# Expert rows weighted before they are stored, and a second attention with a new order of its side work

## The chip, the cores and the metric

One core of a Trainium2 chip runs the kernel. Its engines are TensorE (PE in the profile, its weight loads PEld), VectorE (DVE), ScalarE (ACT), GpSimd (POOL) and SyncE (SP), which here only issues transfers. Each runs its own program; semaphores order them. The metric is the device time of one execution in microseconds, median of three runs.

## What is computed

8192 tokens (128 sequences of 64) of 128 values go through four blocks, each added to x:

```python
x = x + L0_xattn(layernorm(x), ctx_1024, ctx_1024, mask)     # 16 heads of 8
x = x + L0_ffn(layernorm(x))       # rmsnorm, 32 experts, top 4, clipped swiglu; returns its input plus the sum
x = x + L1_xattn(layernorm(x), ctx_1024, ctx_1024)           # the same with rotary embedding, no mask
x = x + L1_ffn(layernorm(x))       # 8 experts, hidden 352, top 2, silu gate
# an experts block: y[token] = sum over its k experts of weight[token, k] * expert_k(row[token])
# weight = softmax of the chosen gate logits
```

## The kernel before

All is written by hand: every engine's program, its order and its semaphores. X (64 tiles of 128 tokens) stays in SBUF. The stages run one behind the other: `attention(0)`, `slots(0)`, `invert(0)`, `experts0()`, then the same for layer 1, then `finish()`.

**attention(layer)** takes two tiles (four sequences) an iteration, 32 iterations, in a software pipeline. Each engine has a `body(i, on)` that does pieces of iteration i and of its neighbours (`on(k)` says whether i + k exists; `nx` is i+1, `ex` i+2, `pv` i-1, `pp` i-2). `bodies` writes out the first eight and the last seven, and loops over the rest in pairs.

- SP loads the context and stores the rows for the experts (L380) into `expert_rows`, 512 B each.
- PE: scores (L782) into four banks U_, for layer 0 the next inputs' transposes, values (L838, L844) of pv, projections (L864, L865) of nx into P_, the rows of pp turned (L914), the maxima of i turned (L793) into R_, the scores turned (L807, L819), in layer 1 the rotated projections (L864, L865 again) into M_, nx's values (L875), pv's output (L885, L889) into R_, the gate of pp (L946) into R_, and in layer 1 the transposes of ex's inputs (L857, L859).
- DVE: statistics of ex's X (L497, L502), the four score maxima (L544), a copy of the turned maxima (L551), the division of pv (L584, L586), in layer 1 the rotary products (L592, cosine, then sine) and their sum (L603), normalisation of ex (L518), addition of the output to X (L639), the logits of pp out of PSUM (L559), its output statistics and its top 8 (L572, L576). R_ is one bank for maxima, output and gate, so each waits until the former is read.
- ACT: copies out of PSUM (L734, L683, L740), the exponentials (L659), the experts' rows (L702) and, in layer 1, half of the spreads (L667). A spread copies queries or keys four times, each masked to one head in four.
- POOL: reciprocal roots (`pow`, L424, L448) and what stands around them, spreads (L429: all four heads in layer 0, two in layer 1), and the keeping of the top 8 (L486, L487).

In layer 1 the result of the experts before is still in `slot_results`, one row for each token and chosen expert. POOL's `gather` fetches it for i+4: it copies the indices (L408), then issues eight indirect gathers (L412), four ahead of the spreads and four behind. DVE's `combine(i, k)` adds them to X for i+3 in four steps k, each two operations x = row * weight + x (L535), one tile each; the steps stand between other work (behind L603, behind L518, behind L559, at the end), and each waits for the former.

**slots** ranks the tokens' choices by expert and gives each a slot in tiles of 128 slots; `wts` are the softmax weights. **invert** finds the token of every slot.

**experts0** has 72 groups of four slot tiles. POOL gathers each tile's rows from `expert_rows` (L1354, four a group, four buffers XE), PE turns them (L1415), multiplies (L1453, L1455), turns the hidden values (L1471) and multiplies again (L1488, L1490); ACT copies and does the gelu; DVE clips (L1523, L1525), multiplies (L1530) and copies the result out of PSUM (L1536); SP stores it to `slot_results`. **experts1** does the same for layer 1 with 36 groups, and fetches and weights its own results at its end and in **finish** (L1260, L1276).

## Time and profile before

| | |
|---|---|
| median of 3 runs | 2034.29 us (2033.54 to 2034.76) |
| the profiled execution | 2034.43 us, of which 2032.6 from first to last instruction |
| mean granted TensorE clock | 0.875 |
| busy: PE, DVE, ACT, POOL | 1551.1, 1210.9, 802.7, 1199.5 us |
| slot results gathered, issue to landing | 2.5 us (median) |

The stages in us from the start of the span: first attention to 396, its slots and inversion to 524, first experts to 923, second attention 926 to 1509, slots and inversion to 1568, second experts and finish to the end.

How to read it: a row of a timeline gives the start, the duration, the engine, the line of the kernel and, in brackets, how long the engine was idle before it and what released it. A row "x2" is two instructions. A share of busy time says little here, since the engines wait for each other in turn; the question at each stage is which wait ends last. Matmuls' ends are modelled, so starts are the safer numbers.

### The profile page before, as it was taken

The page shows a single profiled execution, that of the slowest core. Times are in us where ns is not written, and L with a number is a line of the kernel's source. Part 1 is how long each engine was busy: PE and PEld are TensorE (multiplying, and loading weights), DVE is VectorE, ACT ScalarE, POOL GpSimd, SP SyncE. Part 2 cuts the span into 40 slices and gives each one's busy share as a digit, 9 for nine tenths or more (in the row PEclk, how much of TensorE's full clock was granted, in tenths as well). Part 3 has the DMA queues.
Part 4 walks back from the last instruction along what each step waited for, and adds up shares of the span by engine and source line. Part 5 has one row for each costly group of instructions (what it writes and reads, how often), then busy time and mean ns, then how long its engine had stood idle before and what let it go on. Part 6 is the DMA issues. An engine that isn't in the chain of part 4 may idle for free. (4 is left out here: it accounts for less than half of the span.)

```text
span 2032.6 us, 58857 instructions
## 1 busy us (share of the span) xinstructions
PE 1551.1 (76%) x21070; PEld 1134.8 (56%) x21071; DVE 1210.9 (60%) x3027; ACT 802.7 (39%) x1780; POOL 1199.5 (59%) x1657
## 2 busy tenths in 40 slices
PE   1999999609799999982777777787854999998800
PEld 1666666404477777761455555555532777776600
DVE  2677777699455555543788888888768222333312
ACT  1666666516333333321333333333325444444400
POOL 1667666300577777755777777777511634477566
PEclk9999999859899999996888888877775999999955
DMA  5111111000133333362311111111100222233322
GB/s 174 40 32 39 39 39 35 15 2 0 43 104 102 100 97 103 103 78 59 131 47 46 45 47 46 46 46 46 32 12 6 66 60 56 60 88 85 74 63 66
DMA packets 140639, 120.61 MB, mean 59 GB/s; under 512 B 21475, under 2 KB 126731, under 8 KB 140043
## 3 DMA queue, kind: packets, MB, share of 16 engines
q0 software_dynamic: 26112, 53.53, 11.7%
q1 hardware_dynamic: 114206, 65.84, 10.8%
q8 instruction: 55, 0.90, 0.2%
q14 instruction: 26, 0.21, 0.0%
q10 hardware_dynamic: 240, 0.12, 0.0%
HBM read 78.45 MB, written 40.97 MB: 59 GB/s over the span
## 5 line engine op out<-in xcount | busy, mean ns | idle before, releaser
L1354 POOL DMA_INDIRECT arena<-expert_rows,arena x432 | 420.6, 974 | 171.4 <-issue 119.4
L412 POOL DMA_INDIRECT arena<-slot_results,arena x256 | 250.9, 980 | 92.6 <-issue 59.5
L429 POOL TENSOR_TENSOR arena<-arena,head_of 128x1024 f32<-128x1024 f32 (+1 forms) x128 | 187.1, 1482 | 100.4 <-DVE arena L603 52.2
L1694 DVE TENSOR_TENSOR arena<-bank,arena 128x352 f32<-128x352 f32 x144 | 75.5, 524 | 243.9 <-ACT arena L1673 243.8
L1627 PE MATMUL bank<-W,arena 128*128 x576 | 196.8, 465 | 0.9 <-ACT arena L1685 0.9
L1455 PE MATMUL bank<-W,arena 128*128 x576 | 172.9, 396 | 0.0
L659 ACT ACTIVATE arena<-bank 128x512 f32<-128x512 f32 x256 | 132.2, 603 | 101.1 <-PE bank L819 99.2
L544 DVE TENSOR_REDUCE mx<-bank 128x8 f32<-128x512 f32 x256 | 157.8, 678 | 14.5 <-PE bank L782 14.5
L1260 POOL DMA_INDIRECT arena<-slot_results,arena x128 | 122.0, 953 | 55.4 <-issue 26.0
L1523 DVE TENSOR_SCALAR arena<-bank 128x256 f32<-128x256 f32 x144 | 61.1, 424 | 143.8 <-PE bank L1455 143.7
L1641 PEld LDWEIGHTS bank<-W,arena 128*128 128x128 f32 (+1 forms) x864 | 113.3, 191 | 39.4 <-issue 32.2
L1226 PE MATMUL bank<-arena 128*128 128x288 f16 (+1 forms) x384 | 86.1, 394 | 56.7 <-ACT arena L1211 36.3
L946 PE MATMUL bank<-gate_w,arena 128*128 128x32 f32 (+1 forms) x256 | 50.8, 315 | 95.4 <-DVE X L639 94.4
L1641 PE MATMUL bank<-W,arena 128*128 (+1 forms) x864 | 120.8, 276 | 1.9 <-ACT arena L1680 1.9
L535 DVE SCALAR_TENSOR_TENSOR X<-arena,wts,X 128x128 f32 (+1 forms) x256 | 105.2, 451 | 27.2 <-DMA arena<-slot_results,arena 26.0
L734 ACT ACTIVATE arena<-bank 128x512 f32<-128x512 f32 x64 | 38.2, 597 | 206.6 <-PE bank L859 206.6
L1627 PEld LDWEIGHTS bank<-W,arena 128*128 128x128 f32 x576 | 99.5, 193 | 33.0 <-issue 3.1
L1490 PE MATMUL bank<-W,arena 128*128 x576 | 113.8, 318 | 0.0
L584 DVE RECIPROCAL arena<-bank 128x256 f32<-128x256 f32 x64 | 111.8, 1747 | 0.5 <-PE bank L844 0.5
L946 PEld LDWEIGHTS bank<-gate_w,arena 128*128 128x128 f32 x256 | 45.2, 250 | 106.5 <-issue 103.9
L1673 ACT ACTIVATE arena<-bank 128x352 f32<-128x352 f32 x144 | 66.7, 463 | 93.0 <-PE bank L1627 93.0
L782 PE MATMUL bank<-arena 32*64 32x256 f32 x2048 | 97.1, 503 | 4.5 <-POOL arena L429 4.2
(186 smaller groups left out, 3633.0 us busy)
## 6 DMA issues: line engine op xcount, KB each, us to landing
slot_results<-arena SPq DMA_DIRECT2D x108, 256.0 KB
arena<-in_ctx SPq DMA_DIRECT2D x64, 128.0 KB, 2.3
expert_rows<-arena SPq DMA_DIRECT2D x64, 128.0 KB, 2.1
arena<-expert_rows,arena POOLq DMA_INDIRECT x432
arena<-slot_results,arena POOLq DMA_INDIRECT x384, 2.5
W<-in_w SPq DMA_DIRECT2D x1, 4096.0 KB, 12.1
X<-in_x SPq DMA_DIRECT2D x32, 128.0 KB, 2.2
out_x<-arena SPq DMA_DIRECT2D x32, 128.0 KB, 1.8
```

Of the source, the lines that this page charges most:

```text
L412: nc.gpsimd.indirect_dma_start(out=gb[q][:, k * D:(k + 1) * D], out_offset=None, in_=ys, in_offset=bass.IndirectOffsetOnAxis(ap=gi[q][:, k ...
L429: nc.gpsimd.tensor_tensor(dst[i.par].rearrange("p (b j k) -> p b j k", b=4, j=4)[:, :, 0:n, :], src[i.par].rearrange("p (b k) -> p b k", b ...
L535: last = nc.vector.scalar_tensor_tensor(xt, gb[q][:, at:at + D], wts[:, bass.ds(i.n * 2 + j, 1), k], xt, ALU.mult, ALU.add)
L544: nc.vector.tensor_reduce(mx[:].rearrange("p (w c) -> p w c", w=2)[:, :, 32 * r:32 * r + 4], U_[r][:, :].rearrange("p (w j k) -> p w j k", ...
L584: nc.vector.reciprocal(rec, O_[:, 2 * D:4 * D]).then_inc(s["o_recip"], 1)
L659: nc.scalar.activation(Pt[r], U_[r][:, :], ACT.Exp, scale=SCALE).then_inc(s["probs"], 1)
L1260: nc.gpsimd.indirect_dma_start(out=gb[q][:, k * D:(k + 1) * D], out_offset=None, in_=ys, in_offset=bass.IndirectOffsetOnAxis(ap=gi[q][:, k ...
L1354: nc.gpsimd.indirect_dma_start(out=XE[q][:, c * D:(c + 1) * D], out_offset=None, in_=ts, in_offset=bass.IndirectOffsetOnAxis(ap=gi[i.table ...
L1455: last = nc.tensor.matmul(h, XT[i.par][:, c * P:(c + 1) * P], W0a[:, bass.ds(x_e, 1), :], start=False, stop=True, skip_group_check=True)
L1490: last = nc.tensor.matmul(y, AT[pv.par][:, c * P:(c + 1) * P], W0b[:, bass.ds(x_e, 1), :], start=False, stop=True, skip_group_check=True)
L1627: last = nc.tensor.matmul(H_[2 * r + u][:, 0:F1], XT[i.par][:, c * P:(c + 1) * P], W1a[:, bass.ds(x_e, 1), u * F1:(u + 1) * F1], start=Tru ...
L1641: last = nc.tensor.matmul(Y_[j.par][:, d * P:(d + 1) * P], AT[d % 2][0:f, k * P:(k + 1) * P], W1b[0:f, bass.ds(x_e, 1), k * P:(k + 1) * P] ...
```

## The change

In the experts of layer 0 the weights move: `slots(0)` puts each token's four weights and four expert numbers into `pay`, SP stores them behind the token's 128 values in `expert_rows`, whose rows become 136 words (544 B), and `experts0` multiplies a slot's result by its own weight where it left PSUM by a copy before. DVE finds that weight by comparing the row's four expert numbers with the tile's expert, `tile_e`. The experts of layer 1 gather the longer rows too, and keep their weighting at the end.

So the second attention only has to sum four gathered rows. The sum is one reduction and one addition, for i+4, at the end of DVE's body. DVE takes over four small operations of GpSimd. All spreads of layer 1 are made by ScalarE, keys first. The gathers are for i+5 and read `slot` directly; GpSimd's program for layer 1 is written out for every iteration. Rows for the experts, their turning, the gate and its logits are three iterations late instead of two, the choice of the top 8 with them; PE does the gate before nx's values and the output, and the output waits for the logits' copy.

```diff
+ROW = D + 2 * K0
+        pay = sb("pay", [P, TILES, 2 * K0])
+        tile_e = sb("tile_e", [P, SLOT_TILES[0]])
...
-                        sp.dma_start(ts_rows[:, bass.ds(i.n * 2, 2), :],
+                        sp.dma_start(ts_rows[:, bass.ds(i.n * 2, 2), 0:D],
...
-                    def gather(i, half):
+                    def gather(i, k):
+                        if k == 0 and i.n >= 2:
+                            hold(pool, s["combined"], i.n - 1)
+                        for j in range(2):
+                            at, to = i.n * 2 + j, (j * K0 + k) * D
                             nc.gpsimd.indirect_dma_start(
+                                out=gb[i.par][:, to:to + D], out_offset=None, in_=ys,
+                                in_offset=bass.IndirectOffsetOnAxis(ap=slot[:, at, k:k + 1], axis=0),
+                            ).then_inc(gathered[i.par], 16)
...
+                    def body_with_gathers(i, on):
+                        if on(5):
+                            gather(i.at(5), 0)
+                        if on(-2):
+                            scale_outputs(i.at(-2))
+                        if on(5):
+                            gather(i.at(5), 1)
+                        if on(3):
+                            scale_inputs(i.at(3))
+                        if on(5):
+                            gather(i.at(5), 2)
+                        if on(-4):
+                            keep_top(i.at(-4))
+                        if on(5):
+                            gather(i.at(5), 3)
+                    if layer:
+                        for n in range(-5, ITERS + 4):
+                            body_with_gathers(Step(0, n, base), lambda k: 0 <= n + k < ITERS)
...
+                    def combine(i):
+                        q = i.par
+                        hold(dve, gathered[q], (i.half + 1) * 16 * 2 * K0)
+                        nc.vector.tensor_reduce(rows_sum.rearrange("p (i d) -> p i d", i=2),
+                                                gb[q].rearrange("p (i k d) -> p i d k", i=2, k=K0), AX.X, ALU.add
+                                                ).then_inc(s["row_sum"], 1)
+                        hold(dve, s["row_sum"], i.n + 1)
+                        nc.vector.tensor_tensor(tiles(X, i), tiles(X, i), rows_sum.rearrange("p (i d) -> p i d", i=2),
+                                                ALU.add).then_inc(s["combined"], 1)
...
+                    def body_with_sums(i, on):
+                        ex, nx, pv, p3 = i.at(2), i.at(1), i.at(-1), i.at(-3)
+                        if on(3):
+                            hold(dve, s["combined"], i.at(3).n + 1)
+                            stats(i.at(3), small["st_a"], small["mv_a"], "stats_a", "moments_a")
+                        if on(0):
+                            for r in range(UNITS):
+                                score_unit(i, r)
+                            max_rows(i)
+                        if on(-1):
+                            divide(pv)
...
+                            rotate(nx)
+                        if on(-3):
+                            read_logits(p3)
+                        if on(2):
+                            hold(dve, s["rstd_a"], ex.g + 1)
+                            normalise(ex, xn, small["mv_a"], small["rs_a"]).then_inc(s["normed"], 1)
+                        if on(-1):
+                            add_output(pv)
+                        if on(-3):
+                            choose(p3)
+                        if on(-1):
+                            output_stats(pv)
+                        if on(4):
+                            combine(i.at(4))
...
-                            for j in range(pool_heads, 4):
-                                for dst, src in ((Kbd, Kt), (Qbd, Qt)):
+                            for dst, src, done in ((Kbd, Kt, "kbd"), (Qbd, Qt, "qbd")):
+                                for j in range(4):
...
+                    def body_with_rotation(i, on):
+                        ex, nx, pv, p3 = (i.at(k) for k in (2, 1, -1, -3))
+                        if on(0):
+                            scores(i)
+                        if on(-1):
+                            values(pv)
...
+                            projections(nx, P_, wq, wk, s["qk_psum"])
+                        if on(-3):
+                            rows_turned(p3)
...
+                            maxima(i)
+                            turned(i)
...
+                            projections(nx, M_, Wm[:, 8, :], Wm[:, 9, :], s["rot_psum"])
...
+                            gate(p3)
+                        if on(1):
+                            next_values(nx)
+                        if on(-1):
+                            if on(-3):
+                                pe.wait_ge(s["logits"], p3.g + 1)
+                            output(pv)
...
+                            inputs(ex)
...
+                        sp.wait_ge(chain, weighed_at[0])
+                        sp.dma_start(ts_rows[:, :, D:ROW], pay[:]).then_inc(weights_out, 16)
...
+                        if not base:
+                            hold(pool, e["weighed"], i.g - 3)
...
-                            out=XE[q][:, c * D:(c + 1) * D], out_offset=None, in_=ts,
+                            out=XE[q][:, c * ROW:(c + 1) * ROW], out_offset=None, in_=ts,
...
+                    def row_weights(i):
+                        dve.wait_ge(slots_in[i.quad], (i.fourth + 1) * 16 * GROUP)
+                        dve.nop(nofuse=True)
+                        rows = XE[i.quad].rearrange("p (c f) -> p c f", c=GROUP)
+                        ck = lambda v: v.rearrange("p (c k) -> p c k", k=K0)
+                        nc.vector.tensor_tensor(ck(own), rows[:, :, D + K0:ROW],
+                                                tile_e[:, bass.ds(i.n * GROUP, GROUP)].unsqueeze(2)
+                                                .broadcast_to([P, GROUP, K0]), ALU.is_equal).then_inc(e["own"], 1)
+                        dve.wait_ge(e["own"], i.g + 1)
+                        nc.vector.tensor_tensor(ck(own_w), ck(own), rows[:, :, D:D + K0], ALU.mult
+                                                ).then_inc(e["own_w"], 1)
+                        dve.wait_ge(e["own_w"], i.g + 1)
+                        nc.vector.tensor_reduce(row_w[i.quad], ck(own_w), AX.X, ALU.add).then_inc(e["weighed"], 1)
+
                     def body(i, ahead, main, behind):
-                        pv = i.at(-1)
+                        nx, pv = i.at(1), i.at(-1)
+                        if ahead:
+                            row_weights(nx)
...
-                            nc.vector.tensor_copy(YE[pv.par], Y_[:, :]).then_inc(e["y"], 1)
+                            dve.nop(nofuse=True)
+                            nc.vector.tensor_tensor(YE[pv.par].rearrange("p (c d) -> p c d", c=GROUP),
+                                                    Y_[:, :].rearrange("p (c d) -> p c d", c=GROUP),
+                                                    row_w[pv.quad].unsqueeze(2).broadcast_to([P, GROUP, D]), ALU.mult
+                                                    ).then_inc(e["y"], 1)
...
-    ts = nc.dram_tensor("expert_rows", (TOKENS, D), F32, kind="Internal").ap()
+    ts = nc.dram_tensor("expert_rows", (TOKENS, ROW), F32, kind="Internal").ap()
```

## Rows read from the trace of the kernel before

**Rows 1.** Busy us: PE, PEld, DVE, ACT, POOL; then granted clock, DMA.

```profile
926.00:1509.00 583.00, 430.06 (x7968) 307.32 (x7968) 443.69 (x1216) 201.86 (x449) 406.01 (x607) 0.79 0.19 52
```

**Rows 2.** Timeline of DVE, second attention: start, us, instruction, idle before and releaser.

```profile
1210.56 0.42 DVE L551 COPY arena<-bank 128x256 f32<-128x256 f32 x1 [1.28 <-PE bank L793]
...
1214.71 0.69 DVE L603 TENSOR_TENSOR arena<-arena 128x512 f32<-128x512 f32 x1
...
1216.63 1.31 DVE L518 TENSOR_SCALAR arena<-X,arena 128x128 f32 x2
...
1218.39 0.41 DVE L639 TENSOR_TENSOR X<-bank,X 128x256 f32 x1
...
1219.98 0.17 DVE L559 COPY arena<-bank 128x16 f32<-128x16 f32 x1 [1.18 <-PE bank L946]
...
1220.72 0.48 DVE L497 BATCH_NORM_STATS2 arena<-X 128x6 f32 x2
...
1223.65 2.46 DVE L544 TENSOR_REDUCE mx<-bank 128x8 f32<-128x512 f32 x4
...
1227.56 0.42 DVE L551 COPY arena<-bank 128x256 f32<-128x256 f32 x1 [1.45 <-PE bank L793]
```

**Rows 3.** Timeline of PE in the same iteration.

```profile
1210.14 0.38 PE L793 MATMUL bank<-ident,mx 128*128 128x128 f32 x2
...
1212.61 0.70 PE L864 MATMUL bank<-arena,Wm 128*128 128x256 f32 x2
...
1218.95 0.99 PE L946 MATMUL bank<-gate_w,arena 128*128 128x8 f32 x4 [3.25 <-DVE X L639]
```

**Rows 4.** GpSimd by line, 560 to 860 us: busy, mean ns, idle.

```profile
L1354 POOL DMA_INDIRECT arena<-expert_rows,arena x231 | 228.8, 990 | 68.3 <-issue 64.6 <-POOL arena L1337 2.4 <-PE bank L1415 1.2
```

**Rows 5.** Timelines of ScalarE and of GpSimd in the same iteration.

```profile
1215.44 1.70 ACT L667 ACTIVATE arena<-arena,head_of 128x256 f32<-128x256 f32 x4 [0.71 <-DVE arena L603]
...
1215.49 2.12 POOL L429 TENSOR_TENSOR arena<-arena,head_of 128x512 f32<-128x512 f32 x2 [1.15 <-DVE arena L603]
...
1219.11 0.94 POOL L412 DMA_INDIRECT arena<-slot_results,arena  x1 [0.30 <-issue]
```

**Rows 6.** Timeline of DVE, first iterations of the second attention.

```profile
949.69 0.60 DVE L518 TENSOR_SCALAR arena<-X,arena 128x128 f32<-128x128 f32 x2
```

**Rows 7.** Timeline of PE, last iterations of the second attention.

```profile
1486.89 1.12 PE L782 MATMUL bank<-arena 32*64 32x256 f32 x32 [0.28 <-issue]
...
1488.86 1.05 PE L844 MATMUL bank<-arena,den_of 128*32 128x256 f32 x16
```

**Rows 8.** Instructions by line and form, DVE, 1500 to 1600 us.

```profile
L1072 DVE TENSOR_REDUCE arena<-arena 128x64 f32<-128x1024 f32 x2 | 2.4, 1220 | 0.1
...
L1065 DVE TENSOR_TENSOR arena<-bank,arena 128x512 f32<-128x512 f32 x2 | 1.9, 1005 | 0.0
```

**Rows 9.** Busy time of six us behind PE's long gap.

```profile
1219.00:1225.00 6.00, 6.00 (x112) 4.38 (x116) 4.58 (x22) 1.52 (x4) 4.95 (x11) 0.50 0.33 87
```

**Rows 10.** Timeline of PE, first iterations of the second attention.

```profile
972.45 0.69 PE L793 MATMUL bank<-ident,mx 128*128 128x128 f32 x2 [0.58 <-DVE mx L544]
...
976.61 0.70 PE L864 MATMUL bank<-arena,Wm 128*128 128x256 f32 x2
...
997.05 0.66 PE L857 MATMUL bank<-ident,arena 128*128 128x128 f32 x2 [2.39 <-DVE arena L518]
```

**Rows 11.** Timeline of GpSimd, start of the second attention.

```profile
928.45 0.94 POOL L412 DMA_INDIRECT arena<-slot_results,arena  x1 [0.30 <-issue]
```

**Rows 12.** Timelines of DVE, first and last L551 of the second attention.

```profile
973.17 0.42 DVE L551 COPY arena<-bank 128x256 f32<-128x256 f32 x1 [0.78 <-PE bank L793]
...
1491.17 0.42 DVE L551 COPY arena<-bank 128x256 f32<-128x256 f32 x1 [0.60 <-PE bank L793]
```

**Rows 13.** Timelines of PE and of DVE, first experts stage.

```profile
702.94 0.65 PE L1415 MATMUL bank<-ident,arena 128*128 128x128 f32 x4 [0.57 <-DMA arena<-expert_rows,arena]
...
704.89 0.42 DVE L1523 TENSOR_SCALAR arena<-bank 128x256 f32<-128x256 f32 x1 [1.32 <-PE bank L1455]
```

More of the change, by code:

```diff
@@ L360, in bodies @@
                         body(Step(m, c, base), lambda k: True)
-                for n in range(ITERS - 4, ITERS + 3):
+                for n in range(ITERS - 4, ITERS + 4):
                     at(n)
@@ L670, in projections @@
                                         scale=head_of[:, j:j + 1])
+                                last.then_inc(s[done], 1)
                         else:
@@ new lines, in rows_turned, with gate @@
+                    def rows_turned(i):
+                        pe.wait_ge(s["t_ready"], i.g + 1)
+                        for w in range(2):
+                            last = nc.tensor.transpose(M_[:, w * P:(w + 1) * P],
+                                                       t[i.par][:, w * P:(w + 1) * P], ident[:])
+                        last.then_inc(s["tt_psum"], 1)
+                    def gate(i):
+                        pe.wait_ge(s["tt"], i.g + 1)
+                        for w in range(2):
+                            last = nc.tensor.matmul(R_[:, w * n_e:(w + 1) * n_e],
+                                                    tT[i.par][:, w * P:(w + 1) * P], gw, start=True, stop=True)
+                        last.then_inc(s["gate_psum"], 1)
@@ L1543, in experts1 @@
             place[0] = 0
-            XE = [carve(GROUP * D) for _ in range(4)]
+            XE = [carve(GROUP * ROW) for _ in range(4)]
             XT, YE = (carve2(GROUP * D) for _ in range(2))
```

297 lines of the change are left out of this document (138 added, 159 removed).

## Prediction, made before the kernel was run

> **What bounds the kernel now.** I read the page's slices and the busy time by stage first, then one iteration of the second attention on each engine, then the groups of instructions of the first experts stage. The second attention runs from 926 to 1509 us, 583 us for 32 iterations; no engine is full (DVE 444, PE 430, GpSimd 406 us busy) and the granted clock is 0.79 [rows 1]. So the reader should look for a circle of waits. One iteration takes 17.0 us, from one L551 to the next [rows 2]. DVE goes from L551 (1210.56) through the reciprocal, the rotation (L603 ends at 1215.40), a combine, the normalisation (L518), a second combine, and X (L639, ends 1218.80). Only then does PE, idle for 3.25 us, start the gate's matmuls (1218.95) and behind them, in order, the next inputs' transposes, scores, values and projections, until the maxima's transposes free the next L551 [rows 2, 3]. PE's half is 8.5 us, DVE's 8.2 us: the circle alternates, and what stands between L603 and L639, and the gate in front of the inputs, is paid in full.
>
> The first experts stage is bound elsewhere: GpSimd's gathers are busy 228.8 us and between issues 68.3 us of 300 us [rows 4]. It has no room there.
>
> **The change, part by part, in the second attention.** I rebuild the iteration with the new order instead of only subtracting. Let t = 0 be the end of L603.
>
> DVE: read the logits of three iterations before (0.17 us, no wait, since PE has done that gate long before; before, it waited 1.18 us [rows 2]). Then the normalisation: its two L518 took 1.31 us beside GpSimd's spread, but 0.60 us where no spread ran [rows 2, 5, 6]. The spreads leave GpSimd, so I take 0.60: t = 0.65. The Trainium skill (SBUF — State Buffer, the section on the shared port) says that a DVE operation in a two-port mode and a GpSimd operation block each other for the whole instruction; the trace agrees, 1.31 against 0.60 us, and the sum would be the same by either.
>
> PE: the output's matmuls wait for the logits' copy; from L639's end to L946 a release takes 0.15 us, and three matmuls, of which L864's pair is the measure with 0.70, take about 0.7 [rows 2, 3]: they end at t = 1.0. Inputs about 0.8 us more (four transposes; two take 0.38 [rows 3]).
>
> ScalarE now makes all eight copies of the spread. Four took 1.70 us, starting at t = 0.04 [rows 5]. Those of K are first, so the scores can start at t = 1.9, the same moment as the inputs' end; those of Q end at 3.5, long before they are read. Its iteration grows from 6.3 us (202 over 32 [rows 1]) to about 8.2, no bound.
>
> PE from there at full clock: scores and values 3.0 us (1486.89 to 1489.91 [rows 7]), projections about 1.0, rows turned 0.2: ready for the maxima at t = 6.1.
>
> DVE: X at t = 1.1 (0.34 to the next start). Output statistics, choice and input statistics: L497 to L544 is 2.93 us with one pair of combines of 0.6 in it [rows 2], so 2.3; two waits and three little operations that come over from GpSimd, 0.6 (each some 0.1 issued plus a wait). Then the new sum: one reduction of 128x1024 and one addition of 128x256 (0.42 as L639 [rows 2]) instead of eight operations. A contiguous reduction of 128x1024 takes 1.22 us; but this one reads its four terms 512 B apart, and the only operation that reads with such steps, L1065, took 1.005 us for 512 elements where L603 has 0.69 for as many [rows 2, 8]. That is 0.6 ns an element more, so 1.84 us; I take that, because the access is what differs, and keep 1.22 and 2.3 as ends. The Trainium skill (SBUF — State Buffer, its note on cachelines) states that a read which goes to a new 16-byte line each time pays a penalty, which speaks against this reduction; the trace agrees with L1065. Without the rule and without L1065 the sum would be 0.6 us an iteration lower. Together: 1.1 + 0.34 + 2.3 + 0.6 + 2.35 = t 6.7, and the four L544 (2.46 us [rows 2]) end at t = 9.1.
>
> So DVE, not PE, is late at the maxima: PE stands idle from 6.1 to 9.1. Maxima 0.4 us and release, then L551 to L603's end 4.84 us [rows 2]: an iteration of 14.4 us.
>
> **The clock.** That gap of 3.0 us is in a worse place. After the gap of 3.25 us the granted clock is 0.50 for the next 6 us (1.2 instead of 2.4 GHz) [rows 3, 9], and after one of 2.39 us it fell too: L857's pair takes 0.66 us [rows 10]. Before, the slow stretch fell on scores and values. Now it would fall on the maxima's and turned scores' matmuls and the rotated projections, for whose result DVE's sine step waits without slack: L864 and its twin start at 1212.61 and take 1.1 us together, and between 1213.7 and L603 at 1214.71 DVE has only that step. From L793 to L864 is 4.16 us at the low level and 2.47 at the full one [rows 3, 10]: up to 1.7 us an iteration, 2.7 with the projections, 0 if the clock stays. I take 1.2, less than one full slow stretch, since it may not come in every iteration. Period 15.6 us; bounds 13.8 (cheap reduction, full clock) and 17.1.
>
> GpSimd: eight gathers at 1.25 us (0.94 + 0.30 [rows 5]), and what is left of its 12.7 busy us an iteration (406 over 32 [rows 1]) without 7.6 of gathers, 2.12 of spreads and 0.9 of moved small work: 2.1, with gaps 2.3. Together 12.3 us. It starts an iteration when the sum of two tiles earlier is done and has 14.4 or more, so it hides; if it did not, 12.3 is the floor of the period. Writing its program out costs nothing that I can see: the gathers of the stage's first iterations, which are written out already, have the same 0.30 us between them [rows 11]. The gathers' descriptors read `slot` itself instead of a copy.
>
> **Ends of the stage.** Gathers begin at 927.2, one before the row's [rows 11]. DVE's order wants four tile pairs summed before the first scores, not three: 4 x 10.0 + 1.6 = 968, landing 1.7 (the page has 2.5 from a gather's issue), sum 2.35, statistics 1.0, L544 2.5, maxima 0.8: the first L551 at 976.4, before 973.17 [rows 12]. The last three iterations carry no sum, then no statistics, and are short: 6.1 + 0.5 + 4.84 = 11.5 each. The last L551: 976.4 + 28 x 15.6 + 34.5 = 1447.7, before 1491.17 [rows 12]. The drain behind it keeps its chain (values, output, statistics, gate, choice) and pays about 0.5. Gain: 43 us.
>
> **The weighting in the first experts stage.** Rows of 544 B instead of 512 carry weights and experts. DVE's copy of 512 elements out of PSUM becomes a multiplication of as many; L639, an addition with one input in PSUM, and L551, a copy, both take some 0.42 us for 256 [rows 2], so nothing. Three small operations of DVE (0.2 each with their waits) for the next group stand before its clipping; they wait for the same gather that PE waits for, and from that landing (L1415 at 702.94) to the first clipping (704.89) are 1.95 us in which DVE stood idle 1.32 [rows 13], so they hide; without that cover, 0.6 x 72 = 43 us. GpSimd gets one more wait a group, on something an iteration old. As the stage is GpSimd's, anything that lengthens a gather counts 288 times; no row shows a row of 544 B, so -0 (nothing gets shorter) to +0.25 us each is my bound, and I take 0.007, +2 us in all, since the bytes grow by 6% and descriptors by none. The second experts stage gathers 544 B too, under PE. The payload's transfer (8192 pieces of 32 B) has 110 us of slots and inversion behind it. The first attention is unchanged but for stores to rows 544 B apart, for which nobody waits.
>
> **Sum.** The profiled execution took 2034.43 us (span 2032.6), the median is 2034.29. 2034.4 - 43 + 2 = 1993 us.
>
> **Rivals.** (a) The clock stays up or the reduction is cheap: period 13.8 to 14.9, gain 62 to 93: 1943 to 1974, say 1958. For it: PE's work is otherwise dense. Against it: both gaps above. 0.27. (b) The clock falls in every iteration for the whole turned part, or the strided reduction costs 2.3: period 16.4 to 17.1, 2014 to 2034, say 2025. The price is exactly 28 us per 1 us of period. 0.15. (c) Slower: rows of 544 B make GpSimd's gathers longer, in the one stage that it bounds. From 0.15 us a gather (43 us over 288) the gain is gone; at 0.25 us the time is 2063. For it: no slack on GpSimd there [rows 4]. Against: the operation's time has so far been that of its descriptors, 0.94 us undisturbed, from either table. 0.08. (d) The change does not do what it says: the gate, though three iterations late, still holds PE, because the output now waits for the logits' copy, which stands behind the rotation. In my schedule that costs 0.2 us only, as DVE normalises meanwhile; were it a full round trip, 1.2 us more: 2027. 0.04.
>
> **Numbers.** The forecast, 1975 to 2014, has 0.46. The range, to hold 8 in 10, takes most of (a) and (b): 1948 to 2030. Differences of 0.2% (4 us) are about what a measurement tells from none. Faster 0.88: forecast, (a), most of (b) and (d). Same 0.04, from (b). Slower 0.08, (c).
>
> **What would show it.** L551 to L551 in the loop: 15.6 us. L518 as a pair 0.6 us. No DVE wait ahead of L559's successor. The reduction 1.8 us. PE's one large gap ahead of the maxima, about 3 us, and the granted clock low behind it, at the turned scores; the stage's clock near 0.8 again. GpSimd waiting some 2 us an iteration for the sum. Gathers of 544 B at 0.94 us, stage one of the experts unchanged at 5.2 us a group. It is wrong if the gathers lengthen, if the reduction is above 2.3 us, or if ScalarE's spreads, not DVE, are last at the scores.

## The result, and the profile after

The changed kernel takes 2001.8 us (median of 4 runs, 2000.0 to 2005.6) where the kernel before took 2034.5 beside it: ratio 0.984 (95% interval 0.9825 to 0.985), 33 us less. Its profiled execution has a span of 2000.3 us against 2032.6. The forecast was 1993, the range 1948 to 2030.

All of it but about 1 us is in the second attention (the last result of the first experts leaves PSUM at 921.26, before at 922.59). The row below answers to [rows 1], over the same stretch (with us, then busy us of PE, PEld, DVE, ACT, POOL, the granted clock, the DMA share and GB/s):

```profile
926.00:1509.00 583.00, 383.69 (x7987) 283.16 (x7988) 441.93 (x1173) 252.59 (x586) 317.91 (x420) 0.86 0.18 52
```

GpSimd is busy 318 us instead of 406, ScalarE 253 instead of 202, VectorE as before; the clock is 0.86, not 0.79. One iteration of VectorE, the part that answers to [rows 2] (L573 is the old L551, L625 the old L603, L556 the old L518, L630 the old L639, L581 the old L559, L566 the old L544):

```profile
1199.93 0.42 DVE L573 COPY arena<-bank 128x256 f32<-128x256 f32 x1 [0.53 <-PE bank L833]
...
1204.08 0.69 DVE L625 TENSOR_TENSOR arena<-arena 128x512 f32<-128x512 f32 x1
1204.69 0.17 DVE L581 COPY arena<-bank 128x16 f32<-128x16 f32 x1
1204.78 0.59 DVE L556 TENSOR_SCALAR arena<-X,arena 128x128 f32 x2
1205.87 0.42 DVE L630 TENSOR_TENSOR X<-bank,X 128x256 f32 x1 [0.50 <-PE bank L924]
...
1208.10 2.03 DVE L536 TENSOR_REDUCE arena<-arena 128x256 f32<-128x1024 f32 x1
1210.34 0.43 DVE L540 TENSOR_TENSOR X<-X,arena 128x256 f32 x1 [0.21 <-DVE arena L536]
...
1211.93 2.48 DVE L566 TENSOR_REDUCE mx<-bank 128x8 f32<-128x512 f32 x4
1214.95 0.42 DVE L573 COPY arena<-bank 128x256 f32<-128x256 f32 x1 [0.53 <-PE bank L833]
...
1219.60 0.88 DVE L614 SCALAR_TENSOR_TENSOR arena<-bank,bias_t,sin 128x256 f32<-128x256 f32 x2 [1.31 <-PE bank L905]
...
1231.34 0.42 DVE L573 COPY arena<-bank 128x256 f32<-128x256 f32 x1 [0.53 <-PE bank L833]
```

The reader is to see two iterations here, one of 15.0 us (1199.93 to 1214.95) and one of 16.4 (to 1231.34). The logits are read without a wait, the normalisation is down to 0.59 us, and what differs between the two iterations is one wait: 1.31 us before the sine products. TensorE at the same place, which answers to [rows 3]:

```profile
1206.66 1.12 PE L822 MATMUL bank<-arena 32*64 32x256 f32 x32 [0.57 <-ACT arena L706]
...
1210.57 0.38 PE L933 MATMUL bank<-ident,arena 128*128 128x128 f32 x2
1214.47 0.44 PE L833 MATMUL bank<-ident,mx 128*128 128x128 f32 x2 [3.52 <-DVE mx L566]
1214.84 2.01 PE L847 MATMUL bank<-arena 32*64 32x128 f32 x64
1216.59 1.91 PE L859 MATMUL bank<-arena,max_to 32*64 32x256 f32 x32
1218.43 0.70 PE L904 MATMUL bank<-arena,Wm 128*128 128x256 f32 x2
```

TensorE stands idle for 3.52 us before the maxima's transposes, and behind that the turned scores (L847, L859) take 2.01 and 1.91 us. The windows of that stretch and, under it, of the same one in the iteration before, with the columns of [rows 1], show why:

```profile
1214.60:1218.20 3.60, 3.60 (x98) 2.68 (x98) 3.22 (x5) 0.00 (x0) 2.76 (x4) 0.54 0.08 21
1199.50:1203.00 3.50, 3.50 (x104) 2.84 (x104) 3.03 (x5) 0.98 (x3) 2.69 (x4) 1.00 0.07 19
```

The 15.0 us iteration has the full clock, 2.4 GHz, there; the 16.4 us iteration has a granted 0.54, nearly all at 1.2 GHz. The wait before the sine products comes in about two iterations of three, with 1.2 to 2.2 us. Over the 28 iterations behind the first L573 the mean is 16.07 us (17.01 before). The first and the last L573, which answer to [rows 12]:

```profile
975.32 0.42 DVE L573 COPY arena<-bank 128x256 f32<-128x256 f32 x1 [0.78 <-PE bank L833]
...
1458.73 0.43 DVE L573 COPY arena<-bank 128x256 f32<-128x256 f32 x1 [0.59 <-PE bank L833]
```

The last came at 1491.17, so 32.4 us are gained up to here, and the span is 32.3 us shorter: nothing was gained or lost behind it. The gathers of the first experts stage, same columns as [rows 4]:

```profile
L1443 POOL DMA_INDIRECT arena<-expert_rows,arena x232 | 228.6, 985 | 68.6 <-issue 60.9 <-DVE arena L1620 3.4 <-POOL arena L1424 2.4
```

### The profile page after: what moved, and what is told of

Read it like the earlier page. It is cut to its first block and busy times, and to the rows that moved or that the text cites. A ratio compares the mean times of both kernels' runs of the same rounds, so it can differ in the third digit from the quotient of the medians.

```text
span 2000.3 us, 58820 instructions
## 1 busy us (share of the span) xinstructions
PE 1501.8 (75%) x21070; PEld 1109.1 (55%) x21071; DVE 1214.6 (61%) x3147; ACT 850.7 (43%) x1908; POOL 1108.1 (55%) x1465
## 5 line engine op out<-in xcount | busy, mean ns | idle before, releaser
L413 POOL DMA_INDIRECT arena<-slot_results,slot x256 | 247.7, 968 | 192.9 <-DVE X L540 93.9
L698 ACT ACTIVATE arena<-bank 128x512 f32<-128x512 f32 x256 | 132.2, 602 | 224.3 <-PE bank L859 224.3
L566 DVE TENSOR_REDUCE mx<-bank 128x8 f32<-128x512 f32 x256 | 158.4, 681 | 9.6 <-PE bank L822 9.6
L1347 POOL DMA_INDIRECT arena<-slot_results,arena x128 | 122.0, 953 | 55.4 <-issue 26.6
L430 POOL TENSOR_TENSOR arena<-arena,head_of 128x1024 f32<-128x1024 f32 x64 | 119.8, 1893 | 49.1 <-ACT arena L713 49.1
L706 ACT ACTIVATE arena<-arena,head_of 128x256 f32<-128x256 f32 x256 | 105.6, 495 | 38.7 <-DVE arena L625 38.7
L1739 PEld LDWEIGHTS bank<-W,arena 128*128 128x128 f32 x576 | 99.5, 193 | 32.9 <-issue 3.0
L1785 ACT ACTIVATE arena<-bank 128x352 f32<-128x352 f32 x144 | 66.9, 464 | 93.6 <-PE bank L1739 93.6
L833 PE MATMUL bank<-ident,mx 128*128 128x128 f32 x128 | 28.9, 310 | 97.2 <-DVE mx L566 97.2
L1546 PEld LDWEIGHTS bank<-W,arena 128*128 128x128 f32 x576 | 88.6, 194 | 21.5 <-issue 1.4
L1313 PEld LDWEIGHTS bank<-arena 128*128 128x128 f16 x384 | 41.6, 119 | 100.8 <-issue 36.7
L859 PE MATMUL bank<-arena,max_to 32*64 32x256 f32 x2048 | 91.8, 453 | 0.5 <-issue 0.5
```

The lines of the kernel that those rows point to most:

```text
L413: nc.gpsimd.indirect_dma_start(out=gb[i.par][:, to:to + D], out_offset=None, in_=ys, in_offset=bass.IndirectOffsetOnAxis(ap=slot[:, at, k: ...
L430: nc.gpsimd.tensor_tensor(dst[i.par].rearrange("p (b j k) -> p b j k", b=4, j=4), src[i.par].rearrange("p (b k) -> p b k", b=4).unsqueeze( ...
L566: nc.vector.tensor_reduce(mx[:].rearrange("p (w c) -> p w c", w=2)[:, :, 32 * r:32 * r + 4], U_[r][:, :].rearrange("p (w j k) -> p w j k", ...
L698: nc.scalar.activation(Pt[r], U_[r][:, :], ACT.Exp, scale=SCALE).then_inc(s["probs"], 1)
L1313: last = nc.tensor.matmul(total[g][:, 0:NT], by_id[c].rearrange("p (i k s) -> p i k s", i=2, k=K)[:, j, k, :], hot_high[c].rearrange("p (i ...
L1347: nc.gpsimd.indirect_dma_start(out=gb[q][:, k * D:(k + 1) * D], out_offset=None, in_=ys, in_offset=bass.IndirectOffsetOnAxis(ap=gi[q][:, k ...
```

## The experiments

The theory after the result: two terms make 16.07 us. VectorE's own order, with its two waits of 0.5 us for TensorE, takes 15.0, of which 2.67 are the new sum (from L536's start to L540's end), and TensorE's low clock behind its gap adds 1.1 on average. The rivals: the low clock merely coincides with a long iteration; the reduction has cover; the gain came from the gate's new place alone; the longer rows cost something that something else gave back. All ratios are to the kernel before on the same chip; where the text gives a difference between two kernels in us, it is that of their ratios, times 2034.5. "Period" is the mean of the 28 iterations behind the first L573 (or its equal).

| kernel | ratio (95%) | median us | period us |
|---|---|---|---|
| changed | 0.984 (0.9825 to 0.985) | 2001.8 | 16.07 |
| changed, gap filled with 24 matmuls | 0.972 (0.970 to 0.974) | 1978.6 | 14.93 |
| changed, 12 matmuls | 0.983 (0.981 to 0.985) | 2003.8 | 15.84 |
| changed, reduction in address order | 0.972 (0.970 to 0.975) | 1976.9 | 14.99 |
| changed, sum in two additions | 0.967 (0.964 to 0.970) | 1970.8 | 15.03 |
| two additions and 20 matmuls | 0.961 (0.958 to 0.963) | 1954.6 | 14.10 |
| changed, gate put back | 0.996 (0.995 to 0.998) | 2029.9 | 16.83 |
| gate put back and 24 matmuls | 0.979 (0.977 to 0.981) | 1994.0 | 15.35 |
| changed, rows of 768 B | 0.983 (0.981 to 0.985) | 2001.2 | 16.00 |
| before, gap filled with 24 matmuls | 0.987 (0.986 to 0.989) | 2010.1 | 16.08 |
| two additions spread, 10 matmuls | 0.945 (0.943 to 0.947) | 1925.6 | 13.00 |
| two additions spread | 0.944 (0.941 to 0.947) | 1923.6 | 12.90 |

**The clock.** The gap is filled with matmuls into a part of the bank that nobody reads:

```diff
                             pe.wait_ge(s["added"], pv.g)
+                        if on(-2) and on(1):
+                            for _ in range(24):
+                                nc.tensor.matmul(R_[:, 256:512], ones_b[:], sel_of[:, 0:256], start=True, stop=True,
+                                                 skip_group_check=True)
                         if on(0):
                             maxima(i)
```

> The changed kernel, with 24 matmuls of 256 bfloat16 columns, whose result nobody reads, put on TensorE between the wait for the residual and the transposes of the maxima, so that the 3.5 us in which TensorE otherwise idles in every iteration of the second attention are filled. My theory, that the missing 1.2 us between the iterations of 15.0 us at full clock and the mean of 16.2 us are the low clock after that gap: the granted clock of the stage stays at 1.00, the start of L573 returns every 14.9 to 15.2 us in every iteration, and about 29 iterations give back 1.2 us each, some 30 to 35 us, which makes 1965 to 1975 us. Rival one, that the low clock only coincides and the chain through VectorE and the waits on ScalarE is what sets 16.2: within 0.3% of the changed kernel's 2001.8 us. Rival two, that the filler delays the transposes more than it saves (each is 0.11 us at full clock but 0.21 at half): slower, up to 2020 us.

It took 1978.6 us, 24 less than the changed kernel and fewer than the 30 to 35 expected. The period is 1.14 us shorter, 32 us in 28 iterations; but the last three, which have no sum and so no gap, take 39.9 us instead of 33.5, since the idle matmuls stand in their way there (VectorE waits 3.52 and 4.63 us for the maxima), and the first L573 comes 2.2 us later. TensorE in one iteration of it, and the busy time of 1000 to 1400 us:

```profile
1211.70 2.78 PE L1008 MATMUL bank<-sel_of,ones_b 128*128 128x256 bf16 x24
1215.16 0.44 PE L833 MATMUL bank<-ident,mx 128*128 128x128 f32 x2 [0.68 <-DVE mx L566]
1215.53 1.24 PE L847 MATMUL bank<-arena 32*64 32x128 f32 x61
```

```profile
1000.00:1400.00 400.00, 352.00 (x7284) 276.01 (x7272) 344.60 (x922) 204.43 (x475) 248.53 (x332) 1.00 0.20 61
```

The clock is 1.00 throughout (0.90 in that window of the changed kernel), L573 returns every 15.0 us from the sixth iteration on, and the sine products wait no more. The low clock is a cause, worth 1.1 us an iteration; VectorE's path makes 15.0. Half the dose:

> The changed kernel with 12 idle matmuls instead of 24, a dose: 1.3 of the 3.5 us of the gap are filled. 24 made every iteration 15.0 us. If the cost goes by the length of the gap that is left (2.2 us; the two kernels with a shorter sum, whose gap was 2.5 to 2.7 us, kept the clock in about half of their iterations), most iterations are 15.0 us and the time is 1978 to 1986 us; if the whole gap has to be filled, it stays at 1995 to 2002 us.

It did nothing that can be measured against the changed kernel (0.983 against 0.984), and I was wrong to think that the length of what is left of the gap decides. TensorE and the window behind it in two iterations in turn:

```profile
1216.46 0.44 PE L833 MATMUL bank<-ident,mx 128*128 128x128 f32 x2 [2.18 <-DVE mx L566]
...
1231.48 0.44 PE L833 MATMUL bank<-ident,mx 128*128 128x128 f32 x2 [1.97 <-DVE mx L566]
```

```profile
1216.50:1220.00 3.50, 3.50 (x102) 2.82 (x103) 3.04 (x5) 0.89 (x2) 2.57 (x4) 1.00 0.12 30
```

```profile
1231.90:1235.40 3.50, 3.50 (x97) 2.54 (x96) 3.29 (x5) 0.00 (x0) 2.77 (x4) 0.51 0.14 37
```

Behind 2.18 us of idle time the clock stayed at 1.00, behind 1.97 it fell to 0.51.

**How much of this the kernel before had.**

```diff
                             output(i, on)
+                            if on(-2) and on(2):
+                                for _ in range(24):
+                                    nc.tensor.matmul(O_[:, 0:256], ones_b[:], sel_of[:, 0:256], start=True,
+                                                     stop=True, skip_group_check=True)
```

> The kernel before with 24 idle matmuls of 256 bfloat16 columns between the output and the gate, where TensorE idles 3.25 us ([rows 3]). Theory that the low clock behind that gap was on the path of the kernel before too: the clock of the stage goes to about 1.0, the scores, values and denominators behind the gate take 3.3 us instead of the 5.4 us that they take at the low clock, and the iteration of 17.06 us becomes 15.2 to 15.8 us: 40 to 55 us less, 1980 to 1995 us, which is more than the change gained. Rival, that in the kernel before VectorE's order covered it: under 10 us less. The two tell how much of the change's own gain could have been had without it.

It gave 26 us, less than the 40 to 55 expected, but most of what the whole change gave (33): the period of 17.06 became 15.68 to 15.85, and twice two iterations of 17.5 to 18.1 came between. What it ran into stands on GpSimd, whose timeline there has no wait for anybody in an iteration but for its own copy of the indices:

```profile
1194.66 1.09 POOL L412 DMA_INDIRECT arena<-slot_results,arena  x1 [0.79 <-POOL arena L408]
...
1199.55 2.12 POOL L429 TENSOR_TENSOR arena<-arena,head_of 128x512 f32<-128x512 f32 x2
...
1208.21 0.19 POOL L450 TENSOR_TENSOR arena<-arena 128x2 f32<-128x2 f32 x1
```

```profile
1208.68 0.88 ACT L702 ACTIVATE arena<-X,arena 128x128 f32 x2 [3.31 <-POOL arena L450]
...
1209.61 0.44 PE L914 MATMUL bank<-ident,arena 128*128 128x128 f32 x2 [1.45 <-ACT arena L702]
```

L450 is the scale for which ScalarE's rows wait, and TensorE's transposes wait for those. So in the kernel before two bounds lay one behind the other: the circle with its low clock at 17.0 us, and GpSimd at 15.7. That GpSimd bounds here shows also in the first pair of long iterations: one gather started 2.08 us after the end of the one before it, for which the profile shows no reason, TensorE then stood idle for 4.30 us before L914, a gap that no idle matmuls fill, and behind that the clock was low (0.50):

```profile
1130.81 0.94 POOL L412 DMA_INDIRECT arena<-slot_results,arena  x1 [2.08 <-issue]
```

```profile
1144.49 0.69 PE L914 MATMUL bank<-ident,arena 128*128 128x128 f32 x2 [4.30 <-ACT arena L702]
```

**The sum.**

```diff
-                                                gb[q].rearrange("p (i k d) -> p i d k", i=2, k=K0), AX.X, ALU.add
+                                                gb[q].rearrange("p (i d k) -> p i d k", i=2, k=K0), AX.X, ALU.add
```

> The changed kernel with the reduction of L536 reading its 1024 words in the order in which they lie (it then adds four neighbouring words instead of the four gathered rows, so this kernel's sum, and what follows from it, isn't the reference's). Theory that the distance of 128 words between the words of one sum is what makes the reduction 2.03 us: it falls to the 1.22 us of the contiguous reduction of [rows 8], the gap of TensorE shrinks from 3.5 to about 2.7 us, and the time falls by about 0.8 us for each of 32 iterations, some 25 us, to about 1976 us, or lower, to 1945 us, if the shorter gap also keeps the clock up. Rival, that a reduction costs about 2 cycles for each element whatever its order, or that the gathers beside it slow it: the reduction stays at 1.9 to 2.03 us and the time within 0.2% of 2001.8 us.

```profile
L536 DVE TENSOR_REDUCE arena<-arena 128x256 f32<-128x1024 f32 x27 | 32.8, 1215 | 1.5 <-issue 0.4
```

In the 400 us from 1000 on the reduction took 1.215 us (2.016 in the changed kernel), so 0.8 us of its price is the distance between the words, and 24 us went with it. (This kernel's sums are wrong, and so is what follows from them.) Now the same sum, rightly, without a reduction:

```diff
-                        nc.vector.tensor_reduce(rows_sum.rearrange("p (i d) -> p i d", i=2),
-                                                gb[q].rearrange("p (i k d) -> p i d k", i=2, k=K0), AX.X, ALU.add
-                                                ).then_inc(s["row_sum"], 1)
+                        nc.vector.tensor_tensor(pair_sum.rearrange("p (i k) -> p i k", i=2), rows[:, :, 0, :],
+                                                rows[:, :, 1, :], ALU.add).then_inc(s["row_sum"], 1)
+                        hold(dve, s["row_sum"], i.n * 2 + 1)
+                        nc.vector.tensor_tensor(rows_sum.rearrange("p (i d) -> p i d", i=2), halves[:, :, 0, :],
+                                                halves[:, :, 1, :], ALU.add).then_inc(s["row_sum"], 1)
```

> The changed kernel with the reduction of L536 written as two additions, of 512 and of 256 results (rows 0 and 1 of four onto rows 2 and 3, then the two halves). By the rows of the changed kernel an addition of 512 elements (L625) is 0.69 us and one of 256 (L608) 0.42 us, so the sum takes 1.1 us plus about 0.2 us of a wait between them instead of 2.03 us: 0.7 us less for each of 32 iterations. Theory that VectorE's path sets the iteration: 20 to 25 us less, 1977 to 1982 us, and up to 1950 us if the gap of TensorE, then 2.8 us, leaves the clock up more often. Rival, that the rows' sum has cover (GpSimd's gathers for the next iteration wait for it 3.2 us but are not on the path) and something else sets the iteration: under 6 us less.

(`rows` is the buffer seen as two halves of two rows each, `halves` the first sum seen as two.) It gave 34 us, more than the 20 to 25: 0.8 us an iteration of VectorE's path, and the gap of TensorE, now 2.5 to 2.6 us, was followed by the low clock in fewer iterations (iterations of 14.1 to 14.3 us in runs where it stayed up, of 15.0 to 16.8 where it fell). Both together:

> Both edits: the sum in two additions, and 20 idle matmuls in TensorE's gap. Theory that VectorE's path and the low clock are two terms that add: 15.0 less 0.7, about 14.3 us for each iteration, some 55 us less than the changed kernel, 1940 to 1955 us. Rival, that they are one (the shorter sum alone would have kept the clock up, or GpSimd's 12.3 us with its waits becomes the bound): no better than the better of the two alone.

```profile
1209.39 0.69 DVE L539 TENSOR_TENSOR arena<-arena 128x512 f32<-128x512 f32 x1
1210.19 0.43 DVE L542 TENSOR_TENSOR arena<-arena 128x256 f32<-128x256 f32 x1
1210.82 0.42 DVE L545 TENSOR_TENSOR X<-X,arena 128x256 f32 x1 [0.20 <-DVE arena L542]
```

1954.6 us, every iteration of the loop 14.0 to 14.3. From L539's start to L545's end are 1.85 us instead of 2.67. Once the clock is kept up, the sum gives 0.83 us an iteration (14.93 to 14.10), as much as its own path is shorter. The gains, 24 us for the clock and 34 for the sum, make 47 together and not 58, probably since the sum alone had already saved some falls of the clock.

**The gate's place.**

```diff
-                            if on(-3):
-                                pe.wait_ge(s["logits"], p3.g + 1)
                             output(pv)
+                        if on(-3):
+                            if on(-1):
+                                pe.wait_ge(s["added"], pv.g + 1)
+                            gate(p3)
```

VectorE's reading of the logits moves behind the addition of the output accordingly.

> The changed kernel with only the place of the gate put back: TensorE multiplies it after the output and after the wait for the residual, and VectorE reads the logits behind the addition of the residual; it is still the gate of three iterations before, and all other parts of the change stay. Theory that this order, not the lateness, is what took the 1.18 us of idle time before L559 of [rows 2] out of the path: VectorE stands still again for about 1.1 to 1.2 us in every iteration, the iteration of 16.2 us becomes 17.2 to 17.5, and the time rises by 30 to 38 us, to 2032 to 2040 us, as much as the whole change gained. Rival, that the round trip is now hidden, since the gate's rows have lain ready for an iteration and only four small matmuls (0.5 us) stand between: VectorE waits 0.5 us, the time rises by 5 to 15 us.

```profile
1216.11 0.88 DVE L614 SCALAR_TENSOR_TENSOR arena<-bank,bias_t,sin 128x256 f32<-128x256 f32 x2 [1.45 <-PE bank L906]
...
1219.28 0.17 DVE L581 COPY arena<-bank 128x16 f32<-128x16 f32 x1 [0.70 <-PE bank L942]
```

25 us lost of the 33 (0.996 against 0.984). But the wait came back as 0.70 us only, not 1.1 to 1.2: nothing but four small matmuls stands between. The other wait, before the sine products, is the clock's, and it now comes in every iteration. So the rival that the gate's new place is the whole gain nearly holds: without it the rest of the change is worth 8 us (0.996). To part the two:

> The kernel with the gate put back, and 24 idle matmuls in its gap of 3.7 us. With the gate put back VectorE waits 0.70 us before the logits and 1.45 us before the sine products in each iteration (17.05 us). Theory that the first wait is the gate's own price and the second that of the low clock: with the clock kept up the second goes, the iteration is 15.4 to 15.7 us, 0.4 to 0.7 us more than the 15.0 us of the changed kernel with its gap filled, and the time is 1988 to 1999 us. Then of the 28 us that putting the gate back cost, half is its wait and half is that the clock fell in every iteration instead of two in three. Rival, that the whole 28 us are the gate's: the iteration stays near 16.2 us, 2008 us or more.

1994.0 us, every iteration of the loop 15.5 us. The gate's own price is 15.5 less 15.0, about 0.4 to 0.5 us an iteration, 15 us of time (0.979 against 0.972), and the other 10 of the 25 are that of the clock's falls. With the clock kept up in both, the rest of the change without the gate's place is worth 17 us (0.979 against 0.987 of the filled kernel before). What the spreads on ScalarE, the weighting in the experts and the moved small operations are worth one by one was not tried.

**The longer rows.**

```diff
-ROW = D + 2 * K0
+ROW = 192
```

> The changed kernel with the rows that the experts gather made 768 bytes wide instead of 544 (the 56 words added are zeros that nobody reads). It bears on the rival of the longer rows. Theory that a gather's time goes by its 128 descriptors and not by its bytes: L1443 keeps its 0.97 us for each of 420 or so, experts0 ends within 2 us of the changed kernel's 921.3 us, and the time is within 0.2%. Rival, that the bytes cost time: 544 bytes took 0.971 us where 512 took 0.974, so a cost would first be seen here; in proportion to the bytes 232 gathers of 0.985 us would grow to 1.39 us, 94 us more in the stage.

```profile
L1444 POOL DMA_INDIRECT arena<-expert_rows,arena x238 | 226.6, 952 | 70.4 <-issue 60.6 <-PE bank L1505 5.5 <-POOL arena L1425 2.4
```

A gather of 128 rows took 0.952 us at 768 bytes and 0.985 at 544, in the same stretch as above, and the medians over all 432 are 0.946 and 0.944 us. The time is the same too (0.983 and 0.984). The bytes cost nothing on GpSimd.

**A version that beats both.** The two additions (`add_pairs` the first, `add_halves` the second) go where VectorE waited for TensorE anyway, and the one onto the residual (`combine`) ahead of the statistics:

```diff
                                 score_unit(i, r)
+                        if on(4):
+                            add_pairs(i.at(4))
                         if on(0):
                             max_rows(i)
...
+                        if on(4):
+                            add_halves(i.at(4))
                         if on(-1):
                             add_output(pv)
                         if on(-3):
                             choose(p3)
+                        if on(4):
+                            combine(i.at(4))
                         if on(-1):
                             output_stats(pv)
-                        if on(4):
-                            combine(i.at(4))
```

> A version meant to be faster than both: the sum in two additions, the first of them put into VectorE's wait of 0.53 us for the transposed maxima and the second into its wait of 0.50 us for the output, the addition onto the residual ahead of the statistics of the rows (which takes the 0.21 us wait before it and that of 0.27 us behind it away), and 10 idle matmuls in what is left of TensorE's gap. VectorE's iteration of 14.17 us would lose 0.5, 0.4, 0.2 and up to 0.2 us: 12.9 to 13.2 us if VectorE is the bound, some 30 us less than the 1954.6 us of both edits, 1920 to 1930 us. Rival, that GpSimd takes over, which is busy or issuing for 12.1 of 14.17 us: not under 12.9 us either way, so hardly to be told apart. Rival, that the copy of the maxima, 0.1 to 0.2 us later, puts TensorE's chain of softmax, output and scores on the path: 13.6 us or more, 1940 us.

> The same without idle matmuls. TensorE needs about 10.4 us of 13.1 at full clock, so that its gap before the maxima is 1.5 to 2 us. If the clock stays up by itself once the iteration is that dense, it is within 5 us of the kernel with ten idle matmuls; if it falls in two iterations of three as in the changed kernel, it is 25 to 35 us slower, 1950 to 1960 us.

1925.6 us with ten idle matmuls, 1923.6 without: no difference, and 5.6% under the kernel before. VectorE, TensorE and the stage's window without idle matmuls:

```profile
1212.91 2.48 DVE L577 TENSOR_REDUCE mx<-bank 128x8 f32<-128x512 f32 x4
1215.31 0.68 DVE L538 TENSOR_TENSOR arena<-arena 128x512 f32<-128x512 f32 x1
1215.92 0.42 DVE L584 COPY arena<-bank 128x256 f32<-128x256 f32 x1
```

```profile
1215.45 0.44 PE L849 MATMUL bank<-ident,mx 128*128 128x128 f32 x2 [1.37 <-DVE mx L577]
```

```profile
1000.00:1350.00 350.00, 284.93 (x6733) 215.21 (x6733) 319.77 (x960) 208.72 (x485) 262.89 (x334) 1.00 0.25 71
```

L538 fills the 0.53 us in which VectorE had waited for the transposes, the gap of TensorE is 1.37 us, and the clock stays at 1.00 by itself. What bounds these iterations of 12.65 and 13.07 us in turn isn't settled by these runs: GpSimd's gathers now wait for the sum only 5.0 us in these 350 (in the changed kernel 84.2), busy and issuing it takes 324 of them, and VectorE is busy 320.

## Why the prediction held, and where it was off

- **The circle and its price** (a time of 1993 us from a period of 15.6): right in kind. The result is 8.8 us later. The last L573 came at 1458.73 where 1447.7 was forecast, 11.0 us later; the first experts stage cost nothing (it ended 1.3 us earlier in these two traces) instead of 2, and the drain 0.1 instead of 0.5. The first L573 came at 975.32, forecast 976.4; the sum for it has a slip (927.2 + 4 x 10.0 + 1.6 is 968.8, not 968), so that its closeness is in part luck.
- **Output and scores**, t = 1.0 to 6.1: right. With t = 0 at L625's end (1204.77), X begins at 1.10 (forecast 1.1), the scores at 1.89 (1.9), and TensorE is ready for the maxima at 6.2 (6.1). But the inputs end at 1.3, not at 1.8, and what the scores wait for is ScalarE's spread of the keys (L822, 0.57 us idle, by L706; 15.4 us in 400). ScalarE last at the scores was named as a sign of being wrong. It cost nothing here, since TensorE then stands idle for 3.5 us before the maxima, but where that gap is short it can count. The wait of the output for the logits' copy is 0.45 us, so rival (d) fell. The two L556 took 0.59 us (0.60).
- **The reduction**, 1.84 us by L1065's rate [rows 8]: under the size. It took 2.03 us, and the addition behind it waits 0.21 us for its own engine, for which 0.1 stood in the sum: 2.67 instead of 2.35 us. L1065 was no close measure: its steps are 256 B, and its other input lies in PSUM. The Trainium skill (SBUF — State Buffer, its note on cachelines) says that a read that always goes to a new line pays a penalty; the same reduction in address order took 1.215 us, so the trace agrees, and the note's size here is 0.8 us in 1024 elements. Choosing this value over 1.22 was the step that kept the forecast near: rival (a)'s cheap reduction did not come.
- **VectorE's other small steps**, 3.24 us from X's start to the reduction and back to L566 by the forecast: 3.40. With the sum's 0.32 and rounding, L566 ends at t = 9.6, not 9.1, the gap is 3.5 us and not 3.0, and a full-clock iteration 15.0 and not 14.4. This is the term that was mis-sized: 0.6 us of 28 iterations is 17 us.
- **From the maxima to L625**, 4.84 us at full clock: right to the hundredth (1199.93 to 1204.77).
- **The clock**, 1.2 us an iteration (0 to 1.7), not in every iteration, in the turned scores: right in place and size. The wait before the sine products is 1.2 to 2.2 us where it comes, in about two iterations of three, and the stage filled by idle matmuls is 1.14 us an iteration faster. The 1.2 was a choice between the ends, from no rule for how often the clock falls, and none was found since; that it met the mean is in part luck. Of the 17 us above 13 are left, since the mean over 28 iterations includes 14.4 and 13.6 us at the start: 16.07 against 15.6 is 13 us, of which the first L573 gave 1.1 and the last three iterations 1.0 back.
- **GpSimd**, a floor of 12.3 us with slack: right for the changed kernel (a wait of 3.22 us for the sum, 93.6 us in 400). What the prediction did not see is the same engine in the kernel before. With the clock repaired there, it bound at 15.7 us. From [rows 1] and [rows 5] the sum was there to be made: 12.7 us busy, and 0.30 us before each of eight gathers, 15.1. The change took the spreads, the copy of the indices and the small operations from it; with that work on GpSimd the period could not have gone below 15.7, by this trace.
- **The gate** three iterations late: the wait before the logits is gone, as forecast, and putting it back costs 0.4 to 0.5 us an iteration at full clock. The rest of what it cost, to 25 us in all, was the clock's. "28 us per 1 us of period" hides this: a wait added on VectorE can cost more than itself. With it TensorE's gap was 3.7 to 3.8 us and the clock fell in every iteration, without it mostly 3.1 to 3.5 us and in two of three.
- **The rows of 544 bytes** (2 us; rival (c), 0.08): nothing, and 768 bytes nothing either. The multiplication out of PSUM (0.68 us, the copy before 0.69) and the three small operations hid as forecast. On VectorE behind the gather, which answers to [rows 13], they stand ahead of the clipping, whose wait for TensorE is down from 1.32 to 0.77 us:

```profile
702.60 0.68 DVE L1645 TENSOR_TENSOR arena<-bank,arena 128x512 f32<-128x512 f32 x1
703.20 0.21 DVE L1613 TENSOR_TENSOR arena<-arena,tile_e 128x16 f32<-128x16 f32 x1
703.44 0.18 DVE L1617 TENSOR_TENSOR arena<-arena 128x16 f32<-128x16 f32 x1
703.65 0.17 DVE L1620 TENSOR_REDUCE arena<-arena 128x4 f32<-128x16 f32 x1
704.59 0.42 DVE L1631 TENSOR_SCALAR arena<-bank 128x256 f32<-128x256 f32 x1 [0.77 <-PE bank L1546]
```

## What to carry to other kernels

Rebuild the iteration in its new order, engine by engine, and put the steps that lie in no one's way where another engine's answer is awaited: the same two additions were worth 34 us at one place, and 81 us when they and the addition onto the residual were spread over what had been waits (0.984 to 0.944). In the 81 is the clock, which then stays up; with it kept up in both, the spreading alone gave 32 us (0.961 to 0.945). One instruction for eight need not be a gain; a reduction whose terms lie apart cost more than the two additions that do the same. When a change leaves an engine's gap between dense stretches of TensorE, count the gap and the low clock behind it as one price, and test the clock with idle matmuls before taking anything else for the cause.

## What the runs showed of the hardware that was not expected

- The low clock behind the gap costs an iteration of the changed kernel 1.3 to 2.0 us (16.3 to 17.0 against 15.0), but the length of the idle time before it does not tell whether it comes: it came behind 1.97 us and not behind 2.18 in one kernel, came behind 3.52 and 3.29 and not behind 3.25 in another. It did not come in the loop where the gap was 1.4 us or less, or filled with 20 or 24 idle matmuls, as long as no second gap opened (the 4.30 us before L914). What else decides was not found.
- The reduction over words 512 B apart took 1.89 us at the start of the stage, where GpSimd's gathers ran beside it, and 1.99 to 2.05 in the loop, where GpSimd was waiting for all but the first 0.2 us of the one at 1208.10. So GpSimd is not what lengthens it; the Trainium skill (SBUF — State Buffer, "Who interferes with whom") also has no contention for a reduction. In address order it took 1.22 and 1.21. What slows it in the loop stays open.
- An indirect gather of 128 rows took the same 0.95 to 0.99 us of GpSimd whether its rows had 544 or 768 bytes.
